# Two-layer vision tower on one core: output projection of the first attention with centred weights, the residual added by a matrix product with identity minus mean

## The chip, the cores and the metric

One core of a Trainium2 chip. The metric is the device time of one execution in microseconds. Everything is in 32-bit floats.

## The reference

64 images of 3x224x224 become 64 patch tokens and a class token each (65 tokens of 128 features), and pass two layers. Each layer is an attention and a feed-forward part, each followed by a residual sum and a layer norm without learned scale. What the change touches is the last step of the first attention:

```python
out = out.transpose(0, 2, 1, 3).reshape(b, n, dim)
return out @ w_out.T + b_out
...
h = _layernorm(h + _L0_attn_ref(h, ...), axis=-1)      # (x - m) / sqrt(v + eps)
```

The feed-forward part of the first layer is a mixture of 16 experts with top-k routing, the second attention a causal one mixed with a moving average, and the second feed-forward part a Sinkhorn routing over 8 experts.

## The kernel before, in words

The kernel is written by hand for five engines with semaphores; the order on each engine is the order of the code. The function `embed_and_attend` covers about the first 339 us: patch embedding, first attention, its layer norm, and the routing logits of the first mixture. It works on 16 groups of 4 images. A group's features lie as 128 partitions (features) by 260 columns (4 images of 65 tokens), so the mean over features is a sum over partitions, which is done on TensorE by a product with a 128x128 table of 1/128 (`T("mean")`).

The groups run through a software pipeline (`pipeline`, L93): in iteration g each engine does the scores of group g + 1, the queries and keys of group g + 2, the embedding of group g + 3 and the end of group g - 1. The first four iterations and the last ones are written out, the middle is a loop. On TensorE (L475 to L540) the embedding of group g + 3, 19 products of 128x256, is cut into five pieces (`embed_next`) that are put between the steps which wait for other engines. After the loop the last groups have no embedding left, and `stream(count)` (L542) puts products there whose result nobody reads.

The end of a group is a chain over three engines. The names are those of the trace, with `a_` ahead:

- ScalarE copies the attention's values to `ot` (L305, `save_heads`).
- TensorE multiplies `wo` and `ot` (`output`, or L493 in the loop), signal `y_done`.
- VectorE `residual` (L654 to L657): `z = y + bo + h_feat`, where `h_feat` is the embedding of that group, copied there by GpSimd (L860). Signal `z_ready`.
- TensorE `mean` (L442): product of the mean table and `z` into bank 4.
- VectorE `centre` (L659 to L663): `zc = z - mean`, signal `centred`.
- ScalarE squares `zc` (`sq`, L786); TensorE `var` (L446) multiplies the mean table and `sq`; ScalarE takes the root to `sd` (L790), with a table load ahead of it.
- VectorE `scale` (L665 to L672): reciprocal of `sd` and `hw = zc * rs`.
- TensorE `tail` (L458): four products for the logits and four transposes; VectorE copies the logits (L677), ScalarE the tokens (L801).

An fp32 product shows as two rows on PE and two weight loads on PEld. In the loop, bank 4 holds the mean and then the value projection of the next group (`values`, L436), which is why TensorE waits for `centred` at L502. VectorE's order in the loop (L731 to L759) is shift of the scores, `residual`, `rotate_queries`, `centre`, `shift_gates`, `rotate_keys`, `values`, `scale`, `normalise` and small gate operations, then `tokens` of the group after the next three (L618). After the loop `centre` and `residual` of the last three groups stand between other steps (L761 to L780).

At the start VectorE waits for the two packed inputs `data` and `tables` (L714, L722), makes two small weight tables (L723, L724) and the class token columns (L726, signal `wmade`), and goes on to `tokens` of group 0. In iteration g = -2 it also computes the moving average's kernel (`average_kernel`, L885) with the helper `then`, which puts a wait behind each operation:

```python
def then(ins):
    count[0] += 1
    ins.then_inc(S.step, 1)
    dve.wait_ge(S.step, count[0])
```

## Time and profile before

| what | value |
|---|---|
| median of 3 runs | 682.94 us (680.3 to 683.67) |
| the profiled execution, time | 682.89 us |
| its span, first to last instruction | 680.8 us |
| mean granted TensorE clock | 0.923 |
| busy share of the span: PE, PEld, DVE, ACT, POOL | 86%, 72%, 70%, 50%, 37% |
| instructions | 21099 |

The span is what the rows of the trace lie in; 2.1 us of the execution's time are outside of it. PE is TensorE's products, PEld its weight loads, DVE VectorE, ACT ScalarE, POOL GpSimd. Times in rows are microseconds from the span's start. A granted clock of 1.00 is the level of 2.4 GHz, 0.50 that of 1.2 GHz. A row of the timeline gives the start, the time until the last of its instructions ended, and in brackets the engine's idle time before it with what ended it. Rows of neighbouring instructions of one engine can overlap a little, so a step's cost in a chain is read from start to start.

### The profile page before, as it was taken

To read this page: it belongs to the slowest core of one execution; us is meant where nothing else is said; L and a number is where in the kernel's file an instruction comes from. 1 tells how busy PE (TensorE), PEld (TensorE's weight loads), DVE (VectorE), ACT (ScalarE), POOL (GpSimd) and SP (SyncE) were. 2 spreads that over 40 slices of the span, in tenths; PEclk is the share of its full clock that TensorE was granted. 3 is DMA by queue.
4 is the path that set the end of the run, shared out by engine and by line. 5 is a ranking of instruction groups with operands and counts; after the bars stand their busy time and mean duration, and the time that the engine had idled before them with its cause. 6 is when DMAs were issued, how large, how long until landed. Compare 5 with 4: busy or idle time off the path is not lost. (4 is left out here: it accounts for less than half of the span.)

```text
span 680.8 us, 21099 instructions
## 1 busy us (share of the span) xinstructions
PE 583.3 (86%) x8575; PEld 487.9 (72%) x8575; DVE 478.9 (70%) x1015; ACT 338.1 (50%) x883; POOL 249.1 (37%) x251
## 2 busy tenths in 40 slices
PE   6889999999999999978777979969899999974332
PEld 4778888888888888867675468969777777763322
DVE  0875777887777787885554658758888888943772
ACT  0012444444445354445444448752788888854630
POOL 6344444443333444440102306662355555520001
PEclk9989999999999999988978999979999999975555
DMA  9843323333333329900070078100000000001210
GB/s 353 348 154 126 106 103 116 128 143 142 142 142 142 139 82 190 127 2 2 15 232 13 0 91 132 31 1 3 3 3 0 0 0 1 4 2 41 71 47 4
DMA packets 36825, 57.49 MB, mean 84 GB/s; under 512 B 19661, under 2 KB 33085, under 8 KB 34269
## 3 DMA queue, kind: packets, MB, share of 16 engines
q1 hardware_dynamic: 36672, 56.61, 29.3%
q8 instruction: 42, 0.69, 0.4%
q14 instruction: 15, 0.12, 0.1%
q0 software_dynamic: 96, 0.07, 0.0%
HBM read 50.13 MB, written 6.54 MB: 83 GB/s over the span
## 5 line engine op out<-in xcount | busy, mean ns | idle before, releaser
L419 PE MATMUL a_bank<-a_x,a_tok_w 128*128 128x256 f32 (+1 forms) x608 | 150.3, 390 | 6.2 <-DMA a_x<-in_x 5.9
L419 PEld LDWEIGHTS a_bank<-a_x,a_tok_w 128*128 128x128 f32 (+1 forms) x608 | 112.9, 192 | 28.2 <-DMA a_x<-in_x 5.9
L854 POOL TENSOR_TENSOR a_qp<-a_cosine,a_swapped 128x260 f32<-128x260 f32 x16 | 15.1, 943 | 172.1 <-DVE a_swapped L639 172.1
L132 POOL TENSOR_TENSOR a_qt<-a_qp,data 128x512 f32<-128x512 f32 x64 | 73.3, 1175 | 2.1 <-POOL a_qp L854 1.7
L290 ACT ACTIVATE a_at<-a_bank 65x256 f32<-65x256 f32 x128 | 39.0, 390 | 24.2 <-PE a_bank L267 24.2
L1301 POOL TENSOR_TENSOR base<-h_tok,bias 65x512 f32<-65x512 f32 x16 | 30.2, 1888 | 38.0 <-ACT h_tok L1284 38.0
L1693 POOL TENSOR_TENSOR yout<-yout,b_inv 128x585 f32<-128x585 f32 (+1 forms) x32 | 35.5, 1111 | 22.7 <-DVE b_inv L1527 22.7
L1607 ACT ACTIVATE yout<-b_bank 65x512 f32<-65x512 f32 x64 | 34.5, 591 | 13.8 <-PE b_bank L1417 13.7
L203 ACT ACTIVATE a_e<-a_e 128x390 f32<-128x390 f32 (+1 forms) x48 | 24.1, 510 | 32.8 <-DVE a_e L183 32.8
L154 PE MATMUL a_bank<-a_kt,a_qt 128*64 128x65 f32 x1024 | 36.4, 233 | 4.2 <-POOL a_qt L137 2.0
L267 PE MATMUL a_bank<-a_mix,a_e 64*65 64x64 f32 x1024 | 38.0, 225 | 2.2 <-ACT a_at L290 2.2
L154 PEld LDWEIGHTS a_bank<-a_kt,a_qt 128*64 128x64 f32 x1024 | 34.1, 147 | 7.0 <-issue 3.4
L180 DVE TENSOR_REDUCE a_mx<-a_bank 128x6 f32<-128x390 f32 (+1 forms) x48 | 25.7, 535 | 19.0 <-PE a_bank L154 18.8
L267 PEld LDWEIGHTS a_bank<-a_mix,a_e 64*65 64x65 f32 x1024 | 33.6, 138 | 6.0 <-issue 3.7
L203 ACT ACT_TABLE_LOAD x14 | 18.0, 1283 | 32.6 <-DVE a_e L183 32.4
L1198 PE MATMUL s_bank<-s_yrows,base 128*65 128x128 f32 x128 | 25.3, 279 | 4.8 <-ACT s_yrows L1266 4.8
L667 DVE RECIPROCAL a_rs<-a_sd 128x260 f32<-128x260 f32 x16 | 28.2, 1765 | 0.0
L1685 POOL TENSOR_TENSOR b_qlast<-b_qm,tables 128x128 f32<-128x128 f32 x16 | 13.7, 857 | 38.7 <-ACT b_qm L1595 38.7
L1698 POOL TENSOR_TENSOR base<-yout,b_means 65x512 f32 (+1 forms) x16 | 16.6, 1037 | 29.8 <-ACT b_means L1626 29.8
L183 DVE TENSOR_TENSOR a_e<-a_bank,a_mx 128x390 f32<-128x390 f32 (+1 forms) x48 | 26.0, 542 | 1.7
L618 DVE SCALAR_TENSOR_TENSOR a_ht<-a_bank,data 128x256 f32<-128x256 f32 x16 | 7.7, 483 | 26.6 <-PE a_bank L419 26.6
L1535 DVE SCALAR_TENSOR_TENSOR yout<-b_bank,blend,base 65x512 f32<-65x512 f32 x16 | 12.0, 747 | 20.5 <-PE b_bank L1399 20.5
(296 smaller groups left out, 1476.8 us busy)
## 6 DMA issues: line engine op xcount, KB each, us to landing
a_x<-in_x SPq DMA_DIRECT2D x14, 2304.0 KB, 7.9
lag_rows<-a_kernel SPq DMA_DIRECT2D x1, 4192.5 KB, 37.7
a_x<-in_x SPq DMA_DIRECT2D x2, 1152.0 KB, 13.6
lags<-lag_rows SPq DMA_DIRECT2D x1, 2112.5 KB
out<-e_plain SPq DMA_DIRECT2D x16, 130.0 KB
expert_weights<-in_w SPq DMA_DIRECT2D x2, 1024.0 KB, 13.2
lags<-lag_rows SPq DMA_DIRECT2D x1, 2047.5 KB
base<-places SPq DMA_DIRECT2D x2, 520.0 KB
```

What stands on the lines that cost most here:

```text
L132: nc.gpsimd.tensor_tensor(qt[:, b * BLOCKS * P:(b + 1) * BLOCKS * P].rearrange("p (c h i) -> p c h i", i=qb, h=HEADS), wide(by_image[:, b, ...
L154: mm = nc.tensor.matmul(o[r * HALF:(r + 1) * HALF, :], qt[:, at_q:at_q + HALF], kt[:, b * TOKENS:(b + 1) * TOKENS], start=True, stop=True)
L180: nc.vector.tensor_reduce(mx[:, s0:s1], raw, AX.X, ALU.max).then_inc(S.max_done, 1)
L183: nc.vector.tensor_tensor(part, raw, wide(mx[:, s0:s1].unsqueeze(2), [P, n, TOKENS]), ALU.subtract).then_inc(S.shifted, 1)
L203: nc.scalar.activation(e[:, s0:s1, :], e[:, s0:s1, :], ACT.Exp, scale=HEAD ** -0.5).then_inc(S.exp_done, 1)
L267: mm = nc.tensor.matmul(mixbanks[r][0:TOKENS, col:col + HALF], e[rows, b * BLOCKS + c, :], mix[rows, :], start=True, stop=True)
L290: nc.scalar.activation(own[:, :, r], mixbanks[r][0:TOKENS, cols].rearrange("t (c h i) -> t c h i", c=BLOCKS, h=HEADS), ACT.Copy).then_inc( ...
L419: mm = nc.tensor.matmul(banks[0][:, 0:GP], w[0:rows, k * DIM:(k + 1) * DIM], x[p][0:rows, k * GP:(k + 1) * GP], start=(k == 0), stop=(k == ...
L667: nc.vector.reciprocal(rs[:, :], sd[:, :]).then_inc(S.inverse, 1)
L1301: nc.gpsimd.tensor_tensor(R.base[0:TOKENS, n, :].rearrange("t (b d) -> t b d", b=GI), tok(n), wide(R.bias1[0:TOKENS, :].unsqueeze(1), [TOK ...
L1607: nc.scalar.activation(own, turnbanks[q][0:TOKENS, :].rearrange("t (b r i) -> t b r i", b=2, r=STRIPS), ACT.Copy).then_inc(S.at_ready, 1)
L1693: nc.gpsimd.tensor_tensor(e[:, part, :], e[:, part, :], wide(inv[:, part].unsqueeze(2), [P, size, TOKENS]), ALU.mult).then_inc(S.probs_rea ...
```

## The change

The mean over features of `z = wo*ot + bo + h_feat` is subtracted by linearity ahead of time. At the start, VectorE makes a copy `wo` with the mean over output features taken out, a table `minus_mean` of identity minus mean, and the centred bias in `means[:, 3:4]`. `output` is now two products into one bank, the first with `minus_mean` and `h_feat`, the second with the centred weights and `ot`, which is added to it. Its result is already centred but for the bias, so `centre` is one VectorE operation that adds the centred bias while it copies out of PSUM. `residual`, the product `mean` and the waits on `z_ready` and `mean_done` are gone, as is the wait on `centred` ahead of `values` in the loop. After the loop, `centre` of group 13 stands where `residual` stood; two filler products ahead of the last mean are gone with it. The packed input `data` has 128 columns more (`bo_all`, the bias in every row; it stands behind `bo1`). Two lists of semaphore names are left out here.

```diff
@@ -70,7 +70,7 @@
              ("gate0", EXPERTS0), ("b1", EXPERTS0), ("b2", EXPERTS0),
              ("wq1", DIM), ("wk1", DIM), ("wv1", DIM), ("bq1", 1), ("bk1", 1), ("bv1", 1),
-             ("wo1", DIM), ("bo1", DIM), ("p1", NDIM), ("q1", NDIM), ("gamma1", NDIM),
+             ("wo1", DIM), ("bo1", DIM), ("bo_all", DIM), ("p1", NDIM), ("q1", NDIM), ("gamma1", NDIM),
              ("adapt", 2), ("gate1", EXPERTS1)]
@@ -341,7 +341,8 @@
         mx, total, inv = sb("mx", [P, SLOTS]), sb("total", [P, SLOTS]), sb("inv", [P, SLOTS])
         at = sb("at", [P, GI, HEADS, TOKENS])
-        ot, z, zc, sq, sd, rs, hw = (sb(n, [P, GT]) for n in ("ot", "z", "zc", "sq", "sd", "rs", "hw"))
+        ot, zc, sq, sd, rs, hw = (sb(n, [P, GT]) for n in ("ot", "zc", "sq", "sd", "rs", "hw"))
+        wo, minus_mean, means = sb("wo", [P, DIM]), sb("minus_mean", [P, P]), sb("means", [P, 4])
         powers, square = sb("powers", [P, TOKENS, NDIM]), sb("square", [P, 2, NDIM])
@@ -439,17 +440,14 @@
                 mm.then_inc(S.v_done, 1)
 
-            def mean(g, bank=4):
-                pe.wait_ge(S.z_ready, g + 1)
-                product(bank, T("mean"), z[:, :]).then_inc(S.mean_done, 1)
-
             def var(g, bank=5):
                 pe.wait_ge(S.squared, g + 1)
                 product(bank, T("mean"), sq[:, :]).then_inc(S.var_done, 1)
 
             def output(g, bank):
+                nc.tensor.matmul(banks[bank][:, 0:GT], minus_mean[:, :], R.h_feat[:, g, :], start=True, stop=False)
                 pe.wait_ge(S.ot_ready, g + 1)
-                product(bank, D("wo"), ot[:, :]).then_inc(S.y_done, 1)
+                nc.tensor.matmul(banks[bank][:, 0:GT], wo[:, :], ot[:, :], start=False, stop=True).then_inc(S.y_done, 1)
 
@@ -489,17 +487,12 @@
                     scores_of_group(nc, g + 1, seq, qt, kt, S)
                 if exists(g - 1):
-                    pe.wait_ge(S.ot_ready, g)
-                    product(5, D("wo"), ot[:, :]).then_inc(S.y_done, 1)
+                    output(g - 1, 5)
                 if exists(g + 2):
                     queries(g + 2, flat)
                 embed_next(0)
-                if exists(g - 1):
-                    mean(g - 1)
                 embed_next(1)
                 if exists(g + 1):
-
-                    wait_past(pe, S.centred, g)
                     values(g + 1, ht[1 - p])
@@ -551,7 +544,6 @@
             output(n - 2, 0)
 
-            pe.wait_ge(S.z_ready, n - 2)
             pe.wait_ge(S.centred, n - 2)
@@ -564,7 +556,6 @@
             values_of_image(nc, 0, at, vs[0], banks[7])
             values_of_image(nc, 1, at, vs[0], banks[7])
-            mean(n - 2, 0)
             pe.wait_ge(S.shifted, 3 * n + 3)
@@ -575,10 +566,10 @@
             pe.wait_ge(S.gate_probs, EARLY)
             turn_gates((EARLY - 1) % 2, late_turned)
+            pe.wait_ge(S.ht_saved, GROUPS)
             output(n - 1, 2)
             mix_last_rows(n, late_bank)
             mix_pair(nc, pe, n, 0, e[1], mix, banks[4:6], S)
-            mean(n - 1, 2)
             pe.wait_ge(S.at_ready, 9 * n + 5)
@@ -594,8 +585,6 @@
             pe.wait_ge(S.sd_ready, n - 1)
             output(n, 0)
-            stream(2)
-            mean(n, 0)
             stream(4)
@@ -651,16 +640,9 @@
                          [TOKENS, GI, HEADS // 2, 2, HEAD]), ALU.add).then_inc(S.v_ready, 1)
 
-            def residual(g, bank=5):
+            def centre(g, bank=5, zc=zc):
                 dve.wait_ge(S.y_done, g + 1)
-                nc.vector.scalar_tensor_tensor(out=z[:, :], in0=banks[bank][:, 0:GT], scalar=D("bo"),
-                                               in1=R.h_feat[:, g, :], op0=ALU.add, op1=ALU.add).then_inc(S.z_ready, 1)
-
-            def centre(g, bank=4, zc=zc):
-
-                dve.wait_ge(S.z_ready, g + 1)
-                dve.wait_ge(S.mean_done, g + 1)
-                nc.vector.tensor_tensor(zc[:, :], z[:, :], banks[bank][:, 0:GT], ALU.subtract).then_inc(S.centred, 1)
+                nc.vector.tensor_scalar(zc[:, :], banks[bank][:, 0:GT], means[:, 3:4], None, ALU.add).then_inc(S.centred, 1)
 
@@ -720,6 +702,12 @@
 
             dve.wait_ge(S.setup, 16)
+            then(nc.vector.tensor_reduce(means[:, 0:1], D("wo"), AX.X, ALU.add))
+            then(nc.vector.tensor_reduce(means[:, 1:2], D("bo_all"), AX.X, ALU.add))
+            then(nc.vector.tensor_scalar(means[:, 0:2], means[:, 0:2], 1.0 / DIM, None, ALU.mult))
+            then(nc.vector.tensor_tensor(means[:, 3:4], D("bo"), means[:, 1:2], ALU.subtract))
+            nc.vector.tensor_tensor(minus_mean[:, :], T("ident"), T("mean"), ALU.subtract).then_inc(S.wo_centred, 1)
+            nc.vector.tensor_scalar(wo[:, :], D("wo"), means[:, 0:1], None, ALU.subtract).then_inc(S.wo_centred, 1)
             nc.vector.tensor_tensor(mix[:, :], D("w_post"), T("same_query"), ALU.mult)
@@ -732,11 +720,9 @@
                     shift_scores(nc, dve, g + 1, seq, e[1 - p], mx, S, 3)
                 if exists(g - 1):
-                    residual(g - 1)
+                    centre(g - 1)
                 if exists(g + 2):
                     rotate_queries(g + 2)
-                if exists(g - 1):
-                    centre(g - 1)
                 if exists(g - 2):
@@ -760,17 +746,14 @@
             n = GROUPS - 1
             shift_scores(nc, dve, n, seq, e[1], mx, S, 3)
-            residual(n - 2, 0)
+            centre(n - 2, 0)
             values(n, 1, tokens_bank)
             normalise(nc, dve, n, e[1], total, inv, S)
-            centre(n - 2, 0)
-            residual(n - 1, 2)
             find_places(EARLY - 1, late_turned)
             keep_place(EARLY - 1)
             scale(n - 2)
             save_logits(n - 2)
             centre(n - 1, 2)
-            residual(n, 0)
 
@@ -2114,6 +2097,7 @@
     put("wo1", a["L1_attn_W_out"])
     put("bo1", every(a["L1_attn_b_out"]))
+    put("bo_all", every(a["L0_attn_b_out"]))
     put("p1", a["L1_attn_p_coeff"])
```

The places at which the steps stand, in the order on the engine. First TensorE in one iteration of the loop, from the scores of group g + 1 (L154, L158) over queries and keys (`a_ht`), embedding (`a_x`) and values (L438) to the variance (`a_sq`); before:

```order
L154 MATMUL a_bank<-a_kt,a_qt 64x65 x32
L158 MATMUL a_bank<-a_kt,a_qt 32x65 x4
L408 MATMUL a_bank<-a_ot,data 128x260
L408 MATMUL a_bank<-a_ht,data 128x260 x2
L419 MATMUL a_bank<-a_x,a_tok_w 128x256 x3
L408 MATMUL a_bank<-a_z,tables 128x260
L419 MATMUL a_bank<-a_x,a_tok_w 128x256 x3
L438 MATMUL a_bank<-data,a_ht 65x128 x4
L408 MATMUL a_bank<-a_sq,tables 128x260
```

The same stretch with the change:

```order
L154 MATMUL a_bank<-a_kt,a_qt 64x65 x32
L158 MATMUL a_bank<-a_kt,a_qt 32x65 x4
L448 MATMUL a_bank<-h_feat,a_minus_mean 128x260
L450 MATMUL a_bank<-a_ot,a_wo 128x260
L409 MATMUL a_bank<-a_ht,data 128x260 x2
L420 MATMUL a_bank<-a_x,a_tok_w 128x256 x6
L439 MATMUL a_bank<-data,a_ht 65x128 x4
L409 MATMUL a_bank<-a_sq,tables 128x260
```

The product with `a_z` is gone from between the two embedding pieces, and one with `h_feat` stands ahead of that with `ot`; three products of 260 columns for the group's end stand in both.

Second, TensorE at the end of the last group, from its output product on (L544 is the filler); before:

```order
L408 MATMUL a_bank<-a_ot,data 128x260
L544 MATMUL a_bank<-tables 128x128 x2
L408 MATMUL a_bank<-a_z,tables 128x260
L544 MATMUL a_bank<-tables 128x128 x4
L408 MATMUL a_bank<-a_sq,tables 128x260
L544 MATMUL a_bank<-tables 128x128 x3
L464 MATMUL a_bank<-data,a_hw 65x16 x4
```

With the change (L537 is the filler):

```order
L448 MATMUL a_bank<-h_feat,a_minus_mean 128x260
L450 MATMUL a_bank<-a_ot,a_wo 128x260
L537 MATMUL a_bank<-tables 128x128 x4
L409 MATMUL a_bank<-a_sq,tables 128x260
L537 MATMUL a_bank<-tables 128x128 x3
L462 MATMUL a_bank<-data,a_hw 65x16 x4
```

The product with `a_z` and its two fillers are gone; the added product stands ahead of the output product.

Third, VectorE at the start, with the change; before, the list begins with `a_mix` (there L723):

```order
L705 TENSOR_REDUCE a_means<-data 128x1
L706 TENSOR_REDUCE a_means<-data 128x1
L707 TENSOR_SCALAR a_means<-a_means 128x2
L708 TENSOR_TENSOR a_means<-data,a_means 128x1
L709 TENSOR_TENSOR a_minus_mean<-tables 128x128
L710 TENSOR_SCALAR a_wo<-data,a_means 128x128
L711 TENSOR_TENSOR a_mix<-data,tables 128x64
L712 TENSOR_TENSOR a_mix_last<-data,tables 128x32
L714 TENSOR_TENSOR a_ht<-data 128x4 x2
L607 SCALAR_TENSOR_TENSOR a_ht<-a_bank,data 128x4x64
```

Six operations stand ahead of the ones that were first, and `tokens` of group 0 (the last row) stands behind all of them.

## Rows read from the trace of the kernel before

**Rows 1.** Windows: us, busy by engine, granted clock, DMA share, GB/s

```profile
66.00:288.00 222.00, 220.53 (x3150) 188.29 (x3152) 177.34 (x384) 103.14 (x223) 90.61 (x96) 1.00 0.46 134
288.00:340.00 52.00, 41.81 (x718) 35.26 (x710) 33.45 (x70) 24.24 (x55) 9.84 (x14) 0.90 0.03 4
```

**Rows 2.** Waits, 66 to 288 us: in total, times, longest

```profile
DVE a_zc L663 <- PE a_bank L408: 4.1, 12, 0.4
```

**Rows 3.** Timeline, one loop group, 174 to 181 us (start, duration)

```profile
174.82 2.09 PE L154 MATMUL a_bank<-a_kt,a_qt 128*64 128x65 f32 x64
...
178.87 0.48 DVE L656 SCALAR_TENSOR_TENSOR a_z<-a_bank,data,h_feat 128x260 f32<-128x260 f32 x1
...
179.26 0.48 DVE L624 SCALAR_TENSOR_TENSOR a_sine<-a_bank,data,tables 128x260 f32<-128x260 f32 x1
...
179.80 0.60 PE L408 MATMUL a_bank<-a_z,tables 128*128 128x260 f32 x2
...
180.24 1.46 PE L419 MATMUL a_bank<-a_x,a_tok_w 128*128 128x256 f32 x6
180.51 0.43 DVE L663 TENSOR_TENSOR a_zc<-a_z,a_bank 128x260 f32<-128x260 f32 x1 [0.37 <-PE a_bank L408]
```

**Rows 4.** Timeline, the start, 15 to 27 us

```profile
15.81 0.22 DVE L723 TENSOR_TENSOR a_mix<-data,tables 128x64 f32<-128x64 f32 x1 [15.81 <-DMA tables<-in_tables]
...
16.05 0.23 DVE L726 TENSOR_TENSOR a_ht<-data 128x4 f32<-128x4 f32 x2
...
17.11 0.48 DVE L618 SCALAR_TENSOR_TENSOR a_ht<-a_bank,data 128x256 f32<-128x256 f32 x1 [0.82 <-PE a_bank L419]
...
22.11 0.17 DVE L892 COPY a_square<-data 128x16 f32<-128x16 f32 x1
...
22.32 0.94 DVE L896 TENSOR_TENSOR a_powers<-a_powers,a_square 128x16 f32<-128x16 f32 x1
...
27.20 1.95 PEld L154 LDWEIGHTS a_bank<-a_kt,a_qt 128*64 128x64 f32 x64 [0.33 <-POOL a_qt L137]
```

**Rows 5.** Timeline, 339 to 355 us: prices of small VectorE operations

```profile
339.00 0.42 DVE L963 TENSOR_REDUCE r_peak<-logits 65x16 f32<-65x256 f32 x1 [0.68 <-PEq L325]
...
339.79 0.28 DVE L965 TENSOR_SCALAR r_wo_bv<-data 128x128 f32<-128x128 f32 x1
...
354.20 0.14 DVE L910 TENSOR_REDUCE r_small<-r_small 128x1 f32<-128x2 f32 x1
```

**Rows 6.** Windows: the DMA's rate at the start

```profile
15.00:16.00 1.00, 1.00 (x7) 0.83 (x5) 0.19 (x2) 0.00 (x0) 0.00 (x0) 1.00 0.99 419
```

**Rows 7.** Timeline, the last group in the loop's order, 292 to 298 us

```profile
292.58 0.48 DVE L656 SCALAR_TENSOR_TENSOR a_z<-a_bank,data,h_feat 128x260 f32<-128x260 f32 x1
...
293.93 0.42 DVE L663 TENSOR_TENSOR a_zc<-a_z,a_bank 128x260 f32<-128x260 f32 x1
...
296.76 0.68 DVE L648 TENSOR_TENSOR a_vs<-a_bank,data 65x512 f32<-65x512 f32 x1
...
297.65 0.27 PE L516 MATMUL a_bank<-a_mix_last,a_e 128*65 128x32 f32 x2 [1.72 <-ACT a_sd L790]
```

**Rows 8.** Timeline, the last group's end, 329 to 339 us

```profile
329.30 0.49 DVE L656 SCALAR_TENSOR_TENSOR a_z<-a_bank,data,h_feat 128x260 f32<-128x260 f32 x1 [1.69 <-PE a_bank L408]
...
329.84 0.71 PE L408 MATMUL a_bank<-a_z,tables 128*128 128x260 f32 x2
...
330.69 0.42 DVE L663 TENSOR_TENSOR a_cosine<-a_z,a_bank 128x260 f32<-128x260 f32 x1 [0.90 <-PE a_bank L408]
...
338.10 0.59 ACT L801 ACTIVATE h_tok<-a_bank 65x512 f32<-65x512 f32 x1 [3.01 <-PE a_bank L467]
```

**Rows 9.** Windows and timeline: TensorE at the lower clock level, 300 to 310 us

```profile
300.00:310.00 10.00, 8.66 (x156) 7.79 (x158) 5.67 (x15) 2.47 (x8) 4.12 (x5) 0.50 0.01 3
...
307.41 3.28 PE L154 MATMUL a_bank<-a_kt,a_qt 128*64 128x65 f32 x64 [0.64 <-DVE a_aff L705]
```

**Rows 10.** Windows: the stretch whose filler products shrink, 321 to 338 us

```profile
321.00:338.00 17.00, 14.92 (x218) 12.69 (x216) 9.46 (x19) 6.87 (x18) 1.21 (x3) 1.00 0.05 5
```

More of the change, by code:

```diff
@@ L318 @@
 ATTN = ("scores_done max_done shifted exp_done summed inverted probs_ready mixed at_ready av_done "
-        "ot_ready y_done z_ready centred squared ")
+        "ot_ready y_done centred squared ")
 def embed_and_attend(nc, A, R):
@@ L329, in embed_and_attend @@
         banks = [ctx.enter_context(nc.psum_tensor(f"a_bank{i}", [P, 512], F32)) for i in range(8)]
-        S = R.first_layer = cleared_later(nc, "a_", ATTN + "mean_done var_done sd_ready inverse h_done setup x0 x1 embedded ht_ready q_done k_done v_done rope_a "
+        S = R.first_layer = cleared_later(nc, "a_", ATTN + "wo_centred var_done sd_ready inverse h_done setup x0 x1 embedded ht_ready q_done k_done v_done rope_a "
                   "rope_ka rope_swapped kt_ready q_sum qt_ready v_ready tail_done tok_saved log_saved feat_saved ht_saved zeroed wmade v_cleared data_in step kernel_done "
```

## The prediction

> **What bounds the kernel now.** I read first the windows of the whole execution. In the long middle of the first attention, 66 to 288 us, TensorE is busy 220.53 of 222 us at the full clock level, VectorE 177.34 us [rows 1]. So twelve groups long nothing but the amount of TensorE work sets the time. The reader is to see in the second window that the last 52 us of this stage are different: TensorE has 41.81 us of work there and the mean granted clock is 0.90. The waits say the same from the other side: in the middle the only wait on the changed chain is VectorE's for the mean product, 4.1 us in 12 times, at most 0.4 us each [rows 2], and no wait of TensorE for `a_z` or `a_zc` has a row there. The timeline of one group shows why: TensorE puts three embedding products between `residual` and the mean product, and three more behind it, which cover VectorE's two steps [rows 3]. Then I read the timeline of the three places without that cover: the start, group 13's iteration (the first without embedding), and the last group's end.
>
> **The change, part by part.** The steady groups: one product of 260 columns goes (mean), one comes (identity minus mean times `h_feat`). From the mean product's start to the next product's start is 180.24 - 179.80 = 0.44 us [rows 3], and the added product has the same shape and number of columns: 0 for TensorE. Both of its inputs are there long before, so its place ahead of the wait for `ot` costs no wait. VectorE loses `residual`, 0.39 us from start to start (179.26 - 178.87), and the wait of 0.37 us for the mean [rows 3]. That makes keys, queries and GpSimd's spreading some 0.8 us earlier, but the scores that use them start when TensorE comes to them. What is late next is again TensorE. Gain 0; the bound on the good side is TensorE's whole idle time, 1.5 us in the 222 us [rows 1], of which none is put down to this chain.
>
> The start: VectorE begins its small tables when the packed inputs have landed, at 15.81 us, is done at 16.05 + 0.23 = 16.28, and then waits 0.82 us for the first embedding, until 17.11 [rows 4]. Only this slack hides the new work. The new work: two sums over 128 elements. A sum with 256 elements in takes 0.42 us, one with 2 takes 0.14 [rows 5]; in between by length, 0.28. The two small ones take about 0.2 each, near the 0.17 of a copy of 16 columns [rows 4]. Each of these four has a wait behind it: from the end of such a copy to the next start is 22.32 - 22.28 = 0.04 us. Then two operations of 128x128 without waits, 0.28 long [rows 5], which overlap to about 0.20 each as the first table operations do. Sum: 2 x 0.32 + 2 x 0.22 + 2 x 0.20 = 1.48 us. `data` grows by 128 columns, 64 KB, ahead of `tables` in the same queue, at 419 GB/s [rows 6]: 0.16 us. VectorE is free at 16.28 + 1.48 + 0.16 = 17.92 and, with the 0.04 behind it, begins `tokens` at about 17.96 where it was 17.11: **0.85 us later**. Nobody catches that up: TensorE waits for this group's queries and keys, VectorE and GpSimd go on from there, and the first scores wait for GpSimd at 27.20 us [rows 4]. Bounds: with sums at 0.14 and the rest at two thirds, 0.3; with sums at 0.42, 1.2. I take 0.85, since 128 elements lie between the two rows.
>
> On this sum a rule of the Trainium skill has another answer: its page "VectorE: DVE Perf Modes", section "The DRAIN you can't avoid", says that a semaphore behind each of a chain of Vector operations costs nothing extra. Here the short operations with a wait stand 0.21 us from start to start at 0.17 long, while of the table operations without a wait two start between 15.81 and 16.05 us, the first alone 0.22 long [rows 4]; by that rule the start would lose some 0.4 us less. I go by the rows.
>
> Group 13's iteration: VectorE is busy from its `residual` at 292.58 without a pause worth naming until the value copy at 296.76 + 0.68 = 297.44, and that copy is what TensorE's next product at 297.65 waits for, though its row names ScalarE's root [rows 7]. In the new order `centre` stands in `residual`'s place and the slot of `centre`, 0.34 us to the next start and under 0.1 us of wait, is gone. The output product now ends 0.44 us later, but VectorE comes to it only at 292.58 with the scores' shift. **0.45 us earlier**; bounds 0 (ScalarE's table load and root take over as what ends last) and 0.9 (that much again).
>
> Next, groups 14 and 15: the added product stands ahead of the mixing of each, 0.44 us later twice, while the removed mean products stood where TensorE waited anyway. Against it, `centre` of group 13 has left the place behind `normalise`, so that the square and the variance product come some 0.3 us earlier. I take +0.1 us; bounds -0.4 and +0.9.
>
> The last group's end: `ot` is the last to come. Before: `residual` at 329.30, mean product 329.84, `centre` 330.69, and from there a rigid chain to the tokens' copy at 338.10 [rows 8]. Now: two products in a row, so `centre` can begin at 329.30 + 0.44 = 329.74 in place of 330.69, **0.95 us earlier**. Fillers are shorter than what they fill. `centre` stays at about 0.42: it still reads 260 columns from PSUM. Bounds 1.2 (no 0.44, if the first product is done while TensorE waits for `ot`; it has little such time) and 0.4.
>
> Sum: 0 + 0.85 - 0.45 + 0.10 - 0.95 = -0.45 us. The profiled execution took 682.89 us, which is within 0.1 us of the median of the runs shown, 682.94: **682.4 us**.
>
> **The rivals.**
> 1. The clock stays up. From 300 to 310 us TensorE runs at 1.2 GHz, 8.66 us busy [rows 9], after an idle time of 1.72 us [rows 7] and others. The 64 score products take 3.28 us there and 2.09 in the middle [rows 3, 9]. If the changed gaps leave the clock at 2.4 GHz, at most 8.66/2 = 4.3 us come back, some 3.8 since ScalarE's steps keep their length: 682.4 - 3.8 = 678.6. Against it: the short waits for `a_z` and `a_zc` in this iteration are filled, but the idle time behind the variance product grows by about as much, since all of it is now done earlier.
> 2. **Slower:** the clock falls at the end. From 321 to 338 us it is full, with 14.92 us busy [rows 10]. Two mean products and two fillers leave this stretch, about 2 us of 14.92, one of them out of a gap in which TensorE waits for ScalarE. If the clock falls there as it does at 300, the remaining work takes twice as long, and up to some 8 us of it (without what only fills) are on the way to the end: 690. It decides by more than 0.5%, 3.9 us over the forecast, if it falls before about 329 us, the middle of the stretch. Against it: no gap there gets as long as the 1.72 us ahead of the fall at 300. The Trainium skill's page "TensorE: The Clock Gate", section "HAM oscillation — how this bites in real kernels", warns of just this, that gaps between bursts of products throttle the array again; this trace has it at 300 us.
> 3. The group's gain reaches the end. If VectorE's 0.39 + 0.37 us were on the way in the 12 middle groups, 9.1 us would go: 673. The 1.5 us of idle time speak against it.
> 4. The change does not shorten the ends: `centre` waits for the product just as long, only the start's 0.85 us stays: 683.7. This is inside "no change".
>
> **How the numbers follow.** The forecast with its bounds and rival 4: 0.80. Rival 1: 0.09. Rival 2: 0.08. Rival 3: 0.03. About 0.5%, 3.4 us, is what a measurement of this kernel can tell from no change, so below 679.5 is faster, above 686.3 slower: faster 0.12, same 0.80, slower 0.08. The bounds of the terms together reach from 681 to 685; a clock that falls or rises a microsecond or two earlier or later widens this below. The range is 679.8 to 684.9 and leaves out rivals 1 to 3.
>
> **What would show it.** Right: VectorE's first `tokens` near 17.96 us and the first scores near 28.0; the middle's idle time unchanged and its groups as long as before; in group 13 the mixing 0.45 us nearer to VectorE's last shift; the last `centre` about 0.1 us behind `y_done` and no second wait. Wrong: a first `tokens` still at 17.1 (the start's term falls), a wait of TensorE in the middle, or a granted clock below 1.00 anywhere between 311 and 338 us, or at 1.00 from 300 to 310.

## The result and the profile after

| what | before | after |
|---|---|---|
| median, run alternately on one chip | 682.12 us (22 runs) | 680.60 us (22 runs) |
| after divided by before | | 0.9971, 95% interval 0.9957 to 0.9985 |
| the profiled execution, its span | 682.89, 680.8 us | 680.64, 678.5 us |
| instructions | 21099 | 21068 |

By the ratio the change saves 2.0 us (1.0 to 2.9): within 0.5% of no change, as forecast, but more than the forecast 0.45 us. Where it comes from, by the same landmarks in both traces (first `tokens` L607 of a group, ScalarE's `ot` of groups 13 and 15, the routing stage's first operation `r_peak`, its last copy `xin`); the last column is the same difference between a copy of either kernel, profiled in one later series:

| stretch | forecast | measured | copies |
|---|---|---|---|
| to `tokens` of the fourth group | +0.85 | +0.65 | +1.80 |
| its twelve groups | 0 | -0.15 | -0.01 |
| group 13's iteration | -0.45 | +1.30 | -0.07 |
| groups 14 and 15, up to the last `ot` | +0.10 | +0.21 | +0.27 |
| last `ot` to `r_peak` | -0.95 | -0.81 | -0.82 |
| routing stage, `r_peak` to last `xin` | 0 | -2.78 | -2.35 |
| all that follows | 0 | -0.68 | -0.51 |

The largest entry is in a stage that the change does not touch. Up to `r_peak` the changed kernel is even 1.20 us behind in the first pair and 1.17 us in the copies, where the forecast has it 0.45 us ahead; all that it saves comes behind that. The last row arises behind 599 us, where the granted clock is at its lower level for a part of the time in every trace; no run takes it apart. First the stages that the change does touch.

The start, timeline after (start, duration, engine; in brackets the idle time before and what ended it):

```profile
15.79 0.29 DVE L705 TENSOR_REDUCE a_means<-data 128x1 f32<-128x128 f32 x1 [15.79 <-DMA tables<-in_tables]
16.11 0.28 DVE L706 TENSOR_REDUCE a_means<-data 128x1 f32<-128x128 f32 x1
16.43 0.17 DVE L707 TENSOR_SCALAR a_means<-a_means 128x2 f32<-128x2 f32 x1
16.63 0.16 DVE L708 TENSOR_TENSOR a_means<-data,a_means 128x1 f32<-128x1 f32 x1
16.82 0.29 DVE L709 TENSOR_TENSOR a_minus_mean<-tables 128x128 f32<-128x128 f32 x1
17.03 0.28 DVE L710 TENSOR_SCALAR a_wo<-data,a_means 128x128 f32<-128x128 f32 x1
17.23 0.22 DVE L711 TENSOR_TENSOR a_mix<-data,tables 128x64 f32<-128x64 f32 x1
...
17.73 0.48 DVE L607 SCALAR_TENSOR_TENSOR a_ht<-a_bank,data 128x256 f32<-128x256 f32 x1
```

Read the starts: the six new operations take 17.23 - 15.79 = 1.44 us (worked out: 1.48), and with the slack of 0.82 us used up, `tokens` stands at 17.73 in place of 17.11 [rows 4]. The tables land at 15.79 us, no later than before; the 0.16 us put down for 64 KB more do not show in this pair. In the copies the step is smaller, 17.36 us for 17.08, because there the inputs land at 15.41 us for 15.96.

The middle, windows of after, columns as in [rows 1]:

```profile
66.00:288.00 222.00, 220.69 (x3140) 188.86 (x3139) 170.12 (x372) 102.67 (x224) 90.68 (x96) 1.00 0.47 134
288.00:340.00 52.00, 40.69 (x716) 35.07 (x714) 31.03 (x62) 23.15 (x54) 8.80 (x11) 0.90 0.04 6
300.00:310.00 10.00, 7.85 (x151) 6.77 (x149) 6.49 (x15) 3.41 (x10) 5.92 (x7) 0.58 0.01 2
312.00:340.00 28.00, 23.48 (x403) 20.36 (x398) 14.91 (x27) 13.96 (x34) 1.21 (x3) 1.00 0.03 4
```

VectorE is busy 170.12 us where it was 177.34 [rows 1]: 7.2 us of its work are gone, and the twelve groups are as long as they were. One group, timeline after:

```profile
177.72 0.71 PE L448 MATMUL a_bank<-h_feat,a_minus_mean 128*128 x2
178.27 0.60 PE L450 MATMUL a_bank<-a_ot,a_wo 128*128 128x260 f32 x2
178.71 1.04 PE L409 MATMUL a_bank<-a_ht,data 128*128 128x260 f32 x4
179.51 0.48 DVE L645 TENSOR_SCALAR a_zc<-a_bank,a_means 128x260 f32<-128x260 f32 x1
179.58 2.75 PE L420 MATMUL a_bank<-a_x,a_tok_w 128*128 128x256 f32 x12
179.90 0.48 DVE L613 SCALAR_TENSOR_TENSOR a_sine<-a_bank,data,tables 128x260 f32<-128x260 f32 x1
```

`centre` stands where `residual` stood and the rotation follows at once, but TensorE's row of products has no gap in which that could show.

Group 13's iteration, and the last group's end, timelines after:

```profile
292.04 1.27 PE L154 MATMUL a_bank<-a_kt,a_qt 128*64 128x65 f32 x35 [2.02 <-issue]
...
294.89 0.48 DVE L645 TENSOR_SCALAR a_zc<-a_bank,a_means 128x260 f32<-128x260 f32 x1
...
299.45 0.28 PE L509 MATMUL a_bank<-a_mix_last,a_e 128*65 128x32 f32 x2 [2.63 <-ACT a_sd L773]
...
331.11 0.60 PE L450 MATMUL a_bank<-a_ot,a_wo 128*128 128x260 f32 x2
331.82 0.49 DVE L645 TENSOR_SCALAR a_cosine<-a_bank,a_means 128x260 f32<-128x260 f32 x1 [2.20 <-PE a_bank L450]
339.30 0.59 ACT L784 ACTIVATE h_tok<-a_bank 65x512 f32<-65x512 f32 x1 [3.01 <-PE a_bank L465]
```

From VectorE's step at 294.89 to the mixing it is 4.56 us, where it was 297.65 - 292.58 = 5.07 [rows 7]: 0.51 less. But ahead of it TensorE stands for 2.02 us for nothing that the profile shows ("issue"), just behind the loop's end, inside the scores. In the trace before the same place has

```profile
289.73 1.26 PE L154 MATMUL a_bank<-a_kt,a_qt 128*64 128x65 f32 x34 [0.17 <-issue]
```

The copies have 1.40 us (before) and 0.93 (changed) there: it scatters between executions of one kernel. The trace has a hint of what TensorE waits for: packets of the kind "instruction", pieces of an engine's program that come by DMA like data. One of queue 8 starts at 289.8 us after, 2.2 us before TensorE goes on, and at 287.1 before. The last `centre` starts 0.11 us behind the end of the output product, without a second wait.

Now the routing stage, which picks the rows of each expert. A store writes the table of places to memory, a load brings it back to every partition (`base`), VectorE makes picking tables (`r_pick`), TensorE multiplies. Timeline before, then after:

```profile
345.81 0.39 SPq L1063 DMA_DIRECT2D places<-r_placef  x1
...
359.73 1.67 DVE L980 TENSOR_SCALAR r_pick<-base,tables 65x512 f32<-65x512 f32 x4 [4.22 <-DMA base<-places]
...
360.27 5.47 PE L1034 MATMUL r_bank<-r_pick,h_tok 128*128 128x128 f32 x32 [2.93 <-DVE r_pick L980]
```

```profile
346.91 0.39 SPq L1046 DMA_DIRECT2D places<-r_placef  x1
...
359.77 1.67 DVE L963 TENSOR_SCALAR r_pick<-base,tables 65x512 f32<-65x512 f32 x4 [3.06 <-DMA base<-places]
360.31 3.84 PE L1017 MATMUL r_bank<-r_pick,h_tok 128*128 128x128 f32 x32 [1.78 <-DVE r_pick L963]
```

From the store's issue to the pick on its data it is 13.92 us before and 12.86 after (13.71 and 13.14 in the copies), with code and data that are the same. TensorE waits 2.93 us before and 1.78 after; the 32 products behind take 5.47 us before, when the clock falls, and 3.84 after. The DMA views of 345 to 356 us tell the traces apart; before:

```profile
q1 hardware_dynamic: 585, 2.43, 69.8%
q8 instruction: 1, 0.02, 0.5%
q14 instruction: 1, 0.01, 0.2%
...
places<-r_placef SPq DMA_DIRECT2D x1, 8.0 KB, 9.2
```

After:

```profile
q1 hardware_dynamic: 604, 2.69, 79.8%
...
places<-r_placef SPq DMA_DIRECT2D x1, 8.0 KB, 8.6
```

Before, two packets of the kind "instruction" fall into these 11 us, after none; the last column is microseconds from issue to landing. The packets of queue 14 start at 342.2 and 350.9 us before, the second inside the store's flight (345.8 to 355.0), and at 343.4 and 366.2 after, on either side of it (346.9 to 355.5). The first stands some 3 us into the stage in every kernel; "the packet" is from here on the other one. That of queue 8 comes at 355.5 us, when the store has landed, and the copy of before has none there.

### The profile page after: what moved, and what is told of

It is laid out like the page before. It is cut to its first block and busy times, and to the rows that moved or that the text cites. A ratio compares the mean times of both kernels' runs of the same rounds, so it can differ in the third digit from the quotient of the medians.

```text
span 678.5 us, 21068 instructions
## 1 busy us (share of the span) xinstructions
PE 581.2 (86%) x8571; PEld 487.2 (72%) x8571; DVE 471.1 (69%) x1005; ACT 337.1 (50%) x883; POOL 249.1 (37%) x251
## 5 line engine op out<-in xcount | busy, mean ns | idle before, releaser
L154 PE MATMUL a_bank<-a_kt,a_qt 128*64 128x65 f32 x1024 | 35.4, 230 | 5.9 <-issue 3.2
L154 PEld LDWEIGHTS a_bank<-a_kt,a_qt 128*64 128x64 f32 x1024 | 33.0, 144 | 8.7 <-issue 5.1
L607 DVE SCALAR_TENSOR_TENSOR a_ht<-a_bank,data 128x256 f32<-128x256 f32 x16 | 7.7, 483 | 34.1 <-PE a_bank L420 34.0
L195 DVE TENSOR_TENSOR a_e<-a_e,a_inv 128x1105 f32<-128x1105 f32 x16 | 25.7, 1606 | 0.5
```

Source lines behind the costliest of these rows:

```text
L154: mm = nc.tensor.matmul(o[r * HALF:(r + 1) * HALF, :], qt[:, at_q:at_q + HALF], kt[:, b * TOKENS:(b + 1) * TOKENS], start=True, stop=True)
```

## The experiments

Ratios are to the kernel before, run alternately with the kernel; the brackets are 95% intervals.

**Copies of both kernels, unchanged.**

> The kernel before once more, unchanged, as a control. The theory that the change is worth what its three places give (start later, group 13 and the last group's end earlier) and that everything else in the first pair of profiles was scatter expects a ratio of 1.000 within 0.002, and a profile whose 338-to-681 part differs from the first profile of before by a microsecond or two (a transfer that lands earlier or later, a stretch of TensorE's clock). The rival, that the further 1.5 us belong to the change, expects this profile to agree with the first one to 0.3 us in the later stages.

> The changed kernel once more, unchanged. By the theory of three places its time stands 0.5 to 1 us below the kernel before (ratio 0.9985 to 0.9993), and its profile has the start 0.6 us later and the last group's end 0.8 us shorter again, while TensorE's 2.0 us of issue idle at 290 us and the earlier end of the routing stage need not come again. By the rival the routing stage is 2.8 us shorter here too and the ratio is 0.997.

Measured: 1.0009 [0.9988, 1.0030] and 0.9965 [0.9944, 0.9986]. The result repeats, and so does its place: the routing stage takes 27.00 and 24.65 us, as the rival of both expectations has it. What does not repeat is the clock at the second scores, at 44 us: at its lower level in the trace before, and full in the copy, which is 1.6 us ahead from there. A single pair of profiles is off by that much. It is not shown, though, that the change has no part in this: the granted clock of 40 to 56 us is 0.89 in the profile before and in those of the changed kernel, its copy, the late set-up, the second centre and the pad of 56, and 1.00 in the copy of before, the set-up alone, the pad of 40, and of changed code without the set-up, with the pad of 24 and with one more product. That is one of four with the code of before and five of eight with the changed code. No run tests whether the later start makes this fall more frequent.

**The set-up alone**, with its wider packed input, added to the kernel before:

```diff
             dve.wait_ge(S.setup, 16)
+            then(nc.vector.tensor_reduce(means[:, 0:1], D("wo"), AX.X, ALU.add))
...
+            nc.vector.tensor_scalar(wo[:, :], D("wo"), means[:, 0:1], None, ALU.subtract).then_inc(S.wo_centred, 1)
```

> The kernel before with the change's six operations and the wider packed input added, their results unused. By the theory of three places: 0.6 us slower than before (ratio 1.001), first tokens at 17.7 us, everything behind it 0.62 us later until TensorE's clock or a transfer makes a difference. The rival, that a shift of the start alone decides which way the clock and the transfers fall, expects a change of 1 us or more in either direction.

Measured: 1.0015 [0.9995, 1.0035]; `tokens` at 18.13 us, 1.02 later than before. The tables landed 0.39 us later than in the trace after, and the sequence from there to `tokens` is 1.95 us long in one and 1.94 in the other. So the start's cost is there and no gain comes with it; the routing stage keeps its 26.92 us.

**The changed kernel without the set-up**:

```diff
-                nc.tensor.matmul(banks[bank][:, 0:GT], minus_mean[:, :], R.h_feat[:, g, :], start=True, stop=False)
+                nc.tensor.matmul(banks[bank][:, 0:GT], T("ident"), R.h_feat[:, g, :], start=True, stop=False)
...
-            then(nc.vector.tensor_reduce(means[:, 0:1], D("wo"), AX.X, ALU.add))
...
-            nc.vector.tensor_scalar(wo[:, :], D("wo"), means[:, 0:1], None, ALU.subtract).then_inc(S.wo_centred, 1)
```

> The changed kernel without its six operations at the start: the products take the identity, the weights and the bias as they come, so the layer norm's mean is not subtracted. If the start's cost is what the profile shows (VectorE's first tokens 0.62 us late, never caught up), this is 0.6 us faster than the changed kernel, ratio to the kernel before 0.998 or less, and the first tokens stand at 17.1 us. If the start's delay is absorbed later, it is as fast as the changed kernel.

Measured: 0.9976 [0.9955, 0.9997], `tokens` at 17.03 us, routing 24.40 us. The first `tokens` waits 1.10 us for TensorE again. Its 0.6 to 0.9 us do not show in the ratio, whose interval is 2.9 us wide.

**The set-up later**, behind `tokens` of the third group, with TensorE's wait for it ahead of the first group's output product:

```diff
+                if isinstance(g, int) and g == 1:
+                    pe.wait_ge(S.wo_centred, 2)
...
+                if isinstance(g, int) and g == -1:
+                    then(nc.vector.tensor_reduce(means[:, 0:1], D("wo"), AX.X, ALU.add))
```

> The changed kernel with its six operations at the start moved behind the first iteration that leaves VectorE idle (after the tokens of group 2, where it waits 2.4 us for the scores), and TensorE's first output product waiting for them. If the start's cost is their place ahead of the first tokens, the first tokens stand at 17.1 us again and the scores of group 1 do not move against them, so this is 0.6 us faster than the changed kernel. If the wider packed input were the cost, the tokens stay at 17.3 us or later.

Measured: 0.9986 [0.9962, 1.0010], `tokens` at 16.83 us, routing 24.37 us. By its profile the start's cost is gone (0.90 us earlier than after); by its time nothing was won. That a late set-up is better is not shown.

**A second `centre` in twelve groups**, VectorE's removed work put back:

```diff
+                if not isinstance(g, int) or g < GROUPS - 4:
+                    nc.vector.tensor_scalar(spare[:, :], banks[bank][:, 0:GT], means[:, 3:4], None, ALU.add)
```

> The changed kernel with a second copy of the centring operation (0.48 us on VectorE) in each of the first 12 groups. If the middle is bound by TensorE, 12 x 0.4 = 4.8 us more VectorE work cost nothing there: ratio to the changed kernel 1.000 within 0.001. If VectorE's time reached the end, 4.8 us, and the removal of residual would have given that much.

Measured: 0.9993 [0.9967, 1.0020]; from the fourth to the sixteenth `tokens` 0.06 us less than in the trace after. By the profile VectorE's work in the groups is free in either direction; the ratio is too wide to tell it from that of the changed kernel or from 1.

**One more product in each group**, that of `minus_mean` and `h_feat` a second time, of 260 columns (the expectation names another shape):

```diff
             def output(g, bank):
+                nc.tensor.matmul(banks[bank][:, 0:GT], minus_mean[:, :], R.h_feat[:, g, :], start=True, stop=True)
```

> The changed kernel with one more product of the mean's matrix over a group's residual (128 x 128 by 128 x 384) in each of the 16 groups, into a bank that the next product clears; the result is unchanged. Theory (TensorE is full from 66 to 288 us, and the change only exchanges one product for another of the same size there): each costs its own duration, about 0.17 to 0.45 us by the rows of the same shape, 3 to 7 us in all, ratio to the kernel before 1.001 to 1.008. Rival (TensorE's fullness there is only waiting that is booked as busy, and VectorE or ScalarE set the pace of the groups): under 1 us, ratio 0.995 to 0.999.

Measured: 1.0064 [1.0040, 1.0087], 6.3 us over the changed kernel's 0.9971, 0.40 each for 16. In the profile twelve groups take 231.81 us against 226.65: 0.43 us each, the 0.44 of [rows 3]. TensorE sets the groups' length, and swapping one product for another is worth nothing.

**A pad of 24 tiny operations on VectorE** in the changed kernel, in the prologue at 42.6 us, 0.38 us in all:

```diff
+                if isinstance(g, int) and g == -1:
+                    for i in range(24):
+                        nc.vector.memset(spare[:, i:i + 1], 0.0)
```

> The changed kernel with 24 one-column memsets on VectorE, hidden in the same idle time near 43 us; they do nothing but make VectorE's code longer again. Theory: in the profiles of the kernel before, a packet of the second instruction queue lands at 350 us, in the middle of the routing stage's transfers, and in those of the changed kernel only at 366 us, because VectorE's code is shorter; the store of places then takes 9.2 or 8.6 us, TensorE waits 2.6 to 2.9 or 1.8 to 2.1 us, and its clock falls or holds. If so, the packet is back near 351 us here, TensorE's last 32 picking products run at the lower level (5.5 us, not 3.8), and the gain of the changed kernel is mostly gone: ratio to before 0.999 to 1.000. The rival, that the earlier end of the routing stage comes from the order of work and not from code length, expects 0.997 and a packet at 366 us.

Measured: 1.0001 [0.9978, 1.0025]. The ratio alone does not show that the saving is gone, since its interval overlaps that of the changed kernel, and the second centre, measured in the same series, has 0.9993. The profile shows what the routing stage lost: up to `r_peak` this execution is 5.2 us ahead of the trace after, at the end only 2.2. The packet lies at 345.8 us, inside the store's flight from 342.0 us, and not near 351 as expected. The DMA view of the pad, 338 to 368 us, and the timeline:

```profile
q14 instruction: 2, 0.02, 0.2%
...
places<-r_placef SPq DMA_DIRECT2D x1, 8.0 KB, 9.1
```

```profile
355.88 1.67 DVE L967 TENSOR_SCALAR r_pick<-base,tables 65x512 f32<-65x512 f32 x4 [4.08 <-DMA base<-places]
356.41 5.47 PE L1021 MATMUL r_bank<-r_pick,h_tok 128*128 128x128 f32 x32 [2.80 <-DVE r_pick L967]
```

**A pad of 40 in the kernel before**, 20 in each of two prologue steps:

```diff
+                if isinstance(g, int) and g in (-1, 0):
+                    for i in range(20):
+                        nc.vector.memset(spare[g + 1][:, i:i + 1], 0.0)
```

> The kernel before, with 40 one-column memsets of a spare tile added on VectorE in the two prologue steps (20 at g == -1, 20 at g == 0), some 0.6 us of VectorE time in all, beside work that TensorE waits for only at the start. Nothing of the attention or the change is touched. Theory (length of VectorE's program sets when its next 16 KB of instructions is fetched, and in the kernel before that fetch falls on the routing stage's transfers, at 350.8 us): the fetch moves some 5 to 20 us away from the store of the places, the store lands after 8.6 us in place of 9.2, TensorE waits about 2.1 us for the last picks in place of 2.7, the last 32 picking products take 3.84 us in place of 5.47, and the time is 0.995 to 0.999 of the kernel before. Rival (the gain in the routing stage belongs to the changed group code, not to the fetch): nothing moves there, the packet may, but the store stays at 9.2 us and the products at 5.47, ratio 1.000 to 1.002. Second rival (the clock there is decided by something else, as with the moved average kernel): the store is 8.6 us and the products are still 5.47, ratio 0.999 to 1.001.

Measured: 0.9982 [0.9958, 1.0007]. The kernel before, lengthened by 40 instructions, has the packet at 329.8 us, ahead of the stage, and its routing stage is as long as in the changed kernel, 24.64 us. Its DMA view, 338 to 368 us, has only the packet that is always there:

```profile
q14 instruction: 1, 0.01, 0.1%
...
places<-r_placef SPq DMA_DIRECT2D x1, 8.0 KB, 8.5
```

Its timeline:

```profile
357.66 3.84 PE L1038 MATMUL r_bank<-r_pick,h_tok 128*128 128x128 f32 x32 [1.32 <-DVE r_pick L984]
```

For the routing stage that refutes the rival by which the gain belongs to the new group code. The ratio alone would not: its interval just takes in 1.

**A pad of 56 in the changed kernel**, 28 in each of the two steps:

```diff
+                if isinstance(g, int) and g in (-1, 0):
+                    for i in range(28):
```

> The changed kernel with 56 one-column memsets of spare tiles on VectorE in the prologue (28 at g == -1, 28 at g == 0), where the earlier pad had 24, at one place. In the profiles of the kernels run so far the store of the places lands after 9.1 or 9.2 us where a packet of queue 14 falls between its issue and its landing (before, its copy, set-up only, before with the kernel moved, the pad of 24), and after 8.5 or 8.6 us where none does (the changed kernel, its copy, and six others). Theory (what the pad costs is where the packet falls, not the memsets): with 56 the packet comes some 6 us after the start of the routing stage, ahead of the store at 7; the store is back at 8.6 us, the wait for the last picks under 2.4, the ratio to the kernel before at 0.996 to 0.9985, and the copy of the changed kernel has 0.9965. Rival (the memsets themselves cost what the pad of 24 lost, 0.38 us of VectorE ahead of the first scores and something behind it): more than twice as many lose at least as much, ratio 1.000 to 1.003.

Measured: 0.9981 [0.9958, 1.0004], the packet at 330.1 us, 7.3 us ahead of the stage and not 6 us into it, the store (issued at 344.3) lands after 8.5 us, a wait of 1.92 us and 3.84 us for the products, routing 24.21 us. More than twice the added work, and the stage's loss is gone: by the profile it is the packet's place that counts.

**The averaging kernel's preparation later**, on the kernel with the late set-up, and on the kernel before:

```diff
-                if isinstance(g, int) and g == -2:
+                if isinstance(g, int) and g == 0:
                     average_kernel(nc, dve, R, (powers, square, kernel), then, S)
```

> The kernel with the late centring, and with the moving average's kernel (9.4 us of VectorE from 21.4 us on) moved two iterations later, ahead of the tokens of group 3, where VectorE waits 5.3 us. TensorE waited 1.7 us for the tokens of group 1 and 2.0 us for the queries of group 1 at the start; both waits go or shrink if VectorE's order is what holds them: 3 us faster than the late centring alone, and up to 1.6 us more if TensorE's clock then does not fall at 44 us. If the tokens of group 3 come too late instead, TensorE waits near 64 us and up to 2 us of it are lost.

> The kernel before, with one edit: the averaging kernel's preparation is moved from the first prologue step to the third (from g == -2 to g == 0). On the changed kernel with its set-up moved late, the same edit gave a ratio of 0.9914 against the kernel before, where the late set-up alone gave 0.9986, so it is put at -0.7 % there. Theory (the averaging kernel stands in front of the first scores' input on VectorE, and that wait at the start also leaves TensorE's clock at its lower level at 44 us; the centring change has no part in it): -3 to -5 us here too, ratio 0.993 to 0.996, TensorE's wait at 40 us shrinks from 3 us and more to about 1, its clock is full at 44 us. Rival (the gain needs the late set-up): ratio 0.998 to 1.001.

Measured: 0.9914 [0.9884, 0.9945] and 0.9943 [0.9920, 0.9965], the two fastest. The second scores, in the trace after and in that of the first of these:

```profile
44.26 1.97 PE L154 MATMUL a_bank<-a_kt,a_qt 128*64 128x65 f32 x52 [1.96 <-POOL a_qt L137]
```

```profile
40.75 2.09 PE L154 MATMUL a_bank<-a_kt,a_qt 128*64 128x65 f32 x64 [0.81 <-POOL a_qt L137]
```

VectorE did this work in front of what TensorE waited for: the scores start 3.5 us earlier, after 0.81 us of waiting, and the granted clock of 40 to 56 us is 1.00 in both where it was 0.89. It is also 1.00 in six profiles without the move, so how much of the gain is clock stays open. The gain does not need the change: 3.9 us (2.4 to 5.5) on the kernel before. The kernel with the late set-up, the moved preparation and the change beats both kernels, by 5.9 us (3.7 to 7.9) against before.

All profiles of the routing stage together, sorted by where the packet lies (us from the span's start; landing, wait, products and stage in us):

| kernel | store issued | packets of queue 14 start | lands after | wait | 32 products | stage |
|---|---|---|---|---|---|---|
| before | 345.8 | 342.2, 350.9 | 9.2 | 2.93 | 5.47 | 26.8 |
| copy of before | 345.6 | 342.0, 350.6 | 9.2 | 2.64 | 5.47 | 27.0 |
| set-up only | 344.9 | 341.3, 350.1 | 9.2 | 2.75 | 5.47 | 26.9 |
| before, preparation late | 343.3 | 339.7, 348.3 | 9.2 | 2.57 | 5.47 | 26.9 |
| pad 24 | 342.0 | 338.4, 345.8 | 9.1 | 2.80 | 5.47 | 26.9 |
| after | 346.9 | 343.4, 366.2 | 8.6 | 1.78 | 3.84 | 24.0 |
| copy of after | 346.6 | 343.1, 366.2 | 8.6 | 2.05 | 3.84 | 24.7 |
| without set-up | 343.3 | 339.7, 363.1 | 8.6 | 2.14 | 3.84 | 24.4 |
| set-up late | 344.4 | 340.8, 364.0 | 8.6 | 2.10 | 3.84 | 24.4 |
| second centre | 343.7 | 340.1, 355.9 | 8.6 | 2.35 | 3.84 | 24.9 |
| before, pad 40 | 344.2 | 329.8, 340.5 | 8.5 | 1.32 | 3.84 | 24.6 |
| pad 56 | 344.3 | 330.1, 340.6 | 8.5 | 1.92 | 3.84 | 24.2 |
| set-up and preparation late | 340.1 | 336.5, 361.2 | 8.6 | 1.98 | 5.47 | 26.2 |
| changed, one more product | 350.2 | 346.6, 371.5 | 8.6 | 1.83 | 5.47 | 26.0 |

In five of five executions with the packet in flight the store takes 0.5 to 0.7 us more and the clock falls behind the wait; in nine without, the store is always at 8.5 or 8.6, and the clock fell in two. The three pads, which only add tiny operations to VectorE's program, switch this in both kernels: off in the kernel before, on and off again in the changed one. So the packet's place is shown to be the cause of the store's later landing. The clock, the larger part of the stage's gain, went the same way with all three pads, but it also fell in two executions without the packet, so the packet is not all that decides it. Behind the five longest waits, 2.57 us and more, the clock fell each time; among the shorter ones their length does not settle it, since waits of 1.98 and 1.83 us were followed by the lower level and one of 2.35 was not. By what way a longer wait brings the clock down is argued and not tested.

Which part of the change moves the packet can be read from its place in the stage. The six operations in front do not: the packet lies 12.2 us behind `r_peak` with the set-up alone, 11.9 and 12.3 in the kernel before and its copy, and 26.6 in the changed kernel without set-up, 26.0 and 26.6 with it. That leaves what the change took out of VectorE's code behind them.

## Why the prediction was right or wrong

**What bounds it: right.** TensorE sets the middle. Two opposite profiles show it: a product more costs its full 0.43 us a group, a VectorE operation more costs nothing. Rival 3 is out.

**The start: right in kind, 0.2 us too large.** `tokens` begins at 17.73 us, 0.62 later and not 0.85; the first scores begin at 27.80, near the 28.0 named. The six operations were sized at 1.48 us and took 1.44: sums of 128 elements 0.29 (0.28 put down), each start to start 0.32 as worked out, the small ones 0.20 (0.22). The DMA term of 0.16 us is not shown: the packed inputs landed 0.02 us earlier than before, and over all profiles they land between 15.35 and 16.18 us, on average at 15.77 in the ten with the wider input and at 15.81 in the four without. By these rows a wait behind a short operation does cost: two sums of 0.28 and 0.29 us with a wait behind each are followed after 0.32 us, while operations of 0.28 and 0.29 us without one are followed after 0.20 and 0.21. They are different operations, so this is a comparison of neighbours and no test. The rule of the Trainium skill's page "VectorE: DVE Perf Modes", section "The DRAIN you can't avoid", that the semaphore costs nothing extra, asked, by the prediction's estimate, for 0.4 us less at the start; the trace does not bear it out here.

**Group 13: the step right (-0.51 for -0.45), the iteration not.** The forecast had no term for the time that TensorE stands behind the loop's exit, 0.17 us in the trace read and from under 0.1 to 2.02 in the others. That it is the change's is not borne out: the copy of before has 1.40 and the set-up alone 1.12, the second centre none. In the eight profiles in which it is over 0.6 us, a packet of queue 8 starts 2.2 to 3.3 us before TensorE goes on. That fits a wait for the next piece of TensorE's program, but no run varies it.

**Groups 14 and 15, and the last end: right**, +0.21 for +0.10, and -0.81 for -0.95. `centre` takes 0.49 us and not 0.42, though it starts as soon as the product is done. Rival 4 is out. So are rivals 1 and 2: the clock was down between 300 and 310 us as before, only from somewhat later on (0.58 for 0.50 [rows 9]), and full from 312 to 340. By the letter the sign against us, a clock below 1.00 between 311 and 338 us, is met, since the fall lasts into that stretch: 0.58 from 311 to 312 us. It is the fall at 300, not the one of rival 2.

**The sum: right as far as it goes, and the result in its range in part by luck.** The measured parts of its own terms, 0.62 at the first `tokens`, -0.51, +0.21 and -0.81, make -0.49 us for the -0.45 forecast; in the copies 0.28, -0.51, +0.27 and -0.82 make -0.78. The times have more in them that the sum lacked: the loop's exit and the clock at 44 us, which put the changed kernel behind up to `r_peak`, and the routing stage, which put it ahead by more. That these left the median at 680.60 us, inside 679.8 to 684.9, was not foreseen. The step that failed was never written out: that what lies outside the attention stays as it is. The change takes a few instructions out of VectorE's loop and ends, and so moves the point at which a further piece of that engine's program is fetched. Before, the fetch fell into the flight of a store for which VectorE and TensorE wait at the end of the routing stage; after, it falls beside it. By packet in flight or not, the ratios are, without the runs with a product more and with the preparation moved:

| | packet in flight | not |
|---|---|---|
| code of before | 1, copy 1.0009, set-up only 1.0015 | pad 40: 0.9982 |
| changed code | pad 24: 1.0001 | 0.9971, copy 0.9965, without set-up 0.9976, pad 56: 0.9981, set-up late 0.9986, second centre 0.9993 |

Along a row the difference is 0.08 to 0.36%, 0.5 to 2.5 us; the profiles show 0.6 us of store and 1.6 us of clock. Down a column, what the change is worth by itself, it is between a loss of 0.11% and a gain of 0.17%, 0.8 and 1.2 us, with each single entry uncertain by some 0.2%. The forecast gain of 0.45 us lies in that; it is not shown more closely, and no change at all lies in it too.

## What to carry to other kernels

Take operations off an engine only where it is waited for: 7.2 us of VectorE work went for nothing, two steps less in a chain with nothing beside it gave 0.8, and moving one block out of the way of TensorE's early inputs gave 3.9 us without any work removed. Before a gain of 0.3% is put down to an edit, look where the profiles differ: if it is in a stage that the edit does not touch, look for instruction packets among its transfers, and run both kernels padded by some tens of tiny operations. Here a change of a few instructions ahead of a store that the engines wait for moved the profiled stage by 2.4 to 2.8 us, more than the edit itself is worth.

## What the runs showed of the hardware

- Instruction packets stand in the trace as packets of queues of their own, those of queue 14 with 8 KB (15 with 0.12 MB in the page; the expectations above say 16 KB). Added VectorE instructions move them: from 26.0 us into the routing stage to 10.8 with 24 more and to 7.3 us ahead of it with 56; in the kernel before from 11.9 us into it to 7.1 ahead of it with 40. With a TensorE product more in each group it was at 28.0, behind the store too. One such packet during a store of 8 KB goes with 9.1 or 9.2 us to its landing in place of 8.5 or 8.6.
- Behind the exit of TensorE's loop an idle time with no releaser ranges from under 0.1 to 2.02 us, for two executions of the kernel before 0.17 and 1.40. Where it is over 0.6 us, an instruction packet of queue 8 starts 2.2 to 3.3 us before its end.
- The granted clock of one and the same stretch differs between executions of a kernel: at 44 us it was at 1.2 GHz in one of two of the kernel before and worth 1.6 us, as much as the whole result.
